# Attention, routing and experts on one core: counting the routing ranks before the output rows, and four other changes of order

## The reference

```
x = layernorm(x + attention(x))       # causal, 16 query heads, 4 key/value heads of 128
x = layernorm(x + ffn(x))

ffn: logits = clip(x @ gate_w.T, -50, 50)            # 8 experts
     top 2 of the logits, rw = softmax of these two
     deltas = softmax(expert_atom_weights) @ atoms ; weighted = deltas * sigmoid(importance)
     each expert adds 4096 scattered entries (positions mask_idx) to the shared matrix W
     out = x @ W.T + sum over the two experts of rw * (their sparse part applied to x)
```

## Time and profile before

| | |
|---|---|
| median of 3 runs | 1902.2 us (1900.52 to 1905.72) |
| the profiled execution | 1894.24 us |
| its span, first to last instruction | 1892.5 us |
| mean granted TensorE clock | 0.981 |
| busy: PE, DVE, ACT, POOL | 92%, 69%, 43%, 41% |
| HBM | 203 GB/s over the span |

### The profile page before, as it was taken

One profiled execution on the slowest core, in us unless ns is written; L12 is line 12 of the kernel. 1 busy time (PEld: TensorE's weight loads), 2 busy tenths in 40 slices (PEclk: granted clock), 3 DMA queues, 4 the chain that ended last, 5 costly groups with the idle time before them and its releaser, 6 DMA issues.

```text
span 1892.5 us, 33146 instructions
## 1 busy us (share of the span) xinstructions
PE 1744.0 (92%) x8750; PEld 1455.4 (77%) x8750; DVE 1313.9 (69%) x4043; ACT 814.2 (43%) x1950; POOL 777.1 (41%) x1093
## 2 busy tenths in 40 slices
PE   8999989998999999999999899999999999999983
PEld 7888877787777777777778777777777778777862
DVE  5566467766777688758876788768776787773356
ACT  4444434434444344434444444444443443434454
POOL 6775444434443322223322333133322224675564
PEclk9999999999999999999999999999999999999997
DMA  9655555555555666556665666576665747544698
GB/s 320 228 206 201 180 174 171 177 159 195 168 168 162 212 210 211 184 187 182 213 201 166 206 211 207 183 232 201 201 195 194 257 134 289 196 156 153 242 313 322
DMA packets 195148, 386.41 MB, mean 204 GB/s; under 512 B 27328, under 2 KB 98144, under 8 KB 184480
## 3 DMA queue, kind: packets, MB, share of 16 engines
q1 hardware_dynamic: 176688, 344.53, 54.0%
q0 software_dynamic: 18288, 39.80, 6.7%
HBM read 261.64 MB, written 122.62 MB: 203 GB/s over the span
## 4 chain that ended last, share of the span: by engine, by line
PE 60%; DVE 15%; issue 10%; ACT 7%; DMA 4%; POOL 2%; DVEq 1%; SPq 1%; ACTq 0%; POOLq 0%
PE psum L1598 17%; PE psum L1600 16%; PE psum L1599 16%; ACT probs L1897 5%; PE psum L1626 4%; DVE probs_blocks L2060 3%; DMA token_rows<-x,ids_now 2%; PE psum L2457 2%; PE psum L2458 2%; PE psum L2459 2%; DVE y_acc L2099 1%; DVE route_product L700 1%; PE psum L376 1%; DMA route_rows<-attn_residual 1%; DVE route_stats L682 1%
## 5 line engine op out<-in xcount | busy, mean ns | idle before, releaser
L1471 POOL TENSOR_SCALAR probs<-probs,row_inv 128x128 f32<-128x128 f32 (+3 forms) x512 | 284.9, 581 | 514.4 <-DVE row_inv L2045 514.1
L1897 ACT ACTIVATE probs<-probs,neg_max 128x512 f32<-128x512 f32 (+3 forms) x512 | 282.0, 553 | 430.6 <-DVE neg_max L2037 429.7
L1598 PE MATMUL psum<-xT_hi,w_hi 128*128 128x512 f32 x640 | 257.4, 402 | 7.8 <-DVE xT_lo L785 3.9
L1600 PE MATMUL psum<-xT_hi,w_lo 128*128 128x512 f32 x640 | 250.8, 392 | 0.0
L1599 PE MATMUL psum<-xT_lo,w_hi 128*128 128x512 f32 x640 | 250.2, 391 | 0.0
L2037 DVE CUSTOM_DVE_ANT_0 probs<-psum,causal 128x512 f32<-128x512 f32 (+3 forms) x512 | 221.3, 487 | 27.3 <-issue 14.2
L1598 PE MATMUL psum<-kT_hi,qT_hi 128*128 128x512 f32 (+3 forms) x512 | 176.4, 345 | 54.6 <-DVE qT_lo L2085 54.6
L1598 PE MATMUL psum<-wo_hi,oT_hi 128*128 128x512 f32 x496 | 198.0, 399 | 26.1 <-DVE y_acc L2099 26.1
L1600 PE MATMUL psum<-wo_hi,oT_lo 128*128 128x512 f32 x496 | 195.4, 394 | 0.0
L1599 PE MATMUL psum<-wo_lo,oT_hi 128*128 128x512 f32 x496 | 194.9, 393 | 0.0
L1599 PE MATMUL psum<-kT_lo,qT_hi 128*128 128x512 f32 (+3 forms) x512 | 169.4, 331 | 0.0
(11 more groups left out here) (255 smaller groups left out, 4037.2 us busy)
## 6 DMA issues: line engine op xcount, KB each, us to landing
w_hi<-split_qk_weights SPq DMA_DIRECT2D x140, 256.0 KB, 3.9
w_lo<-split_qk_weights SPq DMA_DIRECT2D x140, 256.0 KB, 4.8
probs_strips<-probs_blocks SPq DMA_DIRECT2D x54, 640.0 KB, 3.0
probs_moved<-probs_strips SPq DMA_DIRECT2D x216, 160.0 KB, 3.3
wo_hi<-split_out_weights SPq DMA_DIRECT2D x27, 1024.0 KB, 6.5
wo_lo<-split_out_weights SPq DMA_DIRECT2D x27, 1024.0 KB, 8.7
expert_weights_hi_lo<-split_expert_weights SPq DMA_DIRECT2D x8, 2048.0 KB, 10.2
x_in<-in_L_attn_x_dram SPq DMA_DIRECT2D x8, 1024.0 KB, 6.1
```

The lines of the kernel that those rows point to most:

```text
L1471: last = pool.tensor_scalar(p, p, row_inv[:, buf, i:i + 1], 1.0, ALU.mult, ALU.mult)
L1598: pe.matmul(dst, hi_s, hi_m, start=start, stop=False)
L1600: return pe.matmul(dst, lo_s, hi_m, start=False, stop=stop)
L1897: last = act.activation(probs[:, buf, a:a + w], probs[:, buf, a:a + w], ACT.Exp, bias=neg_max[:, buf, i:i + 1], scale=-1.0, accum_out=row_ ...
```

## The change

Ranks and sums: in `first` and `group` iterations of routed batches PE issues `route_ranks` before row 0 instead of after it, and DVE does `route_shares`, `route_ranked` and `route_places` before it adds row 0. The low part of a piece goes from DVE to POOL, after `normalize(n + 4, 0)` and before `route_place`. In every routed iteration but the last, `turn_blocks(n, it, 0)` stands before `qT(n + 2, 0)` on DVE. In `first` iterations of routed batches, variance, normalizing and the first three logits stand behind the maxima of the fourth head, and ACT copies the moved probabilities before it copies the third value row.

More of the change, by code:

```diff
@@ L1851, in iteration @@
                 sum_entries(pe, N, psum, BANKS_PT[0], QUADS_OF[g])
[L1852 to L1855, removed]
+            if route and kind == "batch":
+                ranks()
             if kind == "batch":
@@ L2077, in pT @@
                 low(pT_lo[:, buf, a:z], pT_hi[:, buf, a:z], psum[:, BANKS_PT[u], 0:z - a], s_pt_lo)
-        def low_piece(b, g):
-            dve.wait_ge(s_piece_hi, piece_number(b, g) + 1)
-            low(F.piece_lo[:], F.piece_hi[:], F.piece_raw[:].rearrange("p (r e) -> p e r", e=NE), s_piece_lo)
         def qT(n, buf, bank):
@@ L2180, in iteration @@
                 add_rows(it - 1, 2, "group")
-            if late:
+            if late and not moved:
                 route_normalize(dve, R, tt)
@@ L2198, in iteration @@
                 moved_pT(n, 0)
-            if late:
+            if late and not moved:
                 route_logits(dve, R, tt, (1, 2), products)
+            if late and moved:
+                route_variance(dve, R, tt)
             if kind == "batch" and not moved:
@@ L2277, in iteration @@
                 table_numbers(dve, E, table)
[L2278 to L2284, removed]
+            def ranked():
                 if job == "last" and g == 0:
@@ L2292, in iteration @@
                 route_ranked(dve, R, tt, BANKS_PT[0])
+            if moved and kind != "batch":
+                route_shares(dve, R, tt)
+                ranked()
+                route_places(dve, R, tt)
+            if kind == "first" and route:
+                wait_apart(dve, s_seed, b + 1, s_passed)
+            add_rows(it, 0, banks)
             if kind in ("batch", "end"):
+                add_rows(it, 1, kind)
+                if route:
+                    route_shares(dve, R, tt)
+                    ranked()
                 add_rows(it, 2, kind)
-            if route:
+                if route:
+                    route_places(dve, R, tt)
+                add_rows(it, 3, kind)
+            elif route and not moved:
+                route_shares(dve, R, tt)
+                ranked()
                 route_places(dve, R, tt)
-            if kind in ("batch", "end"):
-                add_rows(it, 3, kind)
         run(dve, iteration)
```

## The result

The changed kernel takes 1883.4 us (median of 5 runs, 1880.9 to 1890.5) against 1902.2 us before: a ratio of 0.991, 95% interval 0.988 to 0.993. It is faster by 0.9%, or 18.8 us, three times the 0.3% that the prediction named as what a measurement can tell from no change. The forecast was 1906 us, no change, with a range of 1892 to 1920, and the result lies under it. The profiled execution took 1885.93 us (span 1884.2, granted clock 0.980).

The account below looks back on a forecast made before the run. PE, busy 92%, was taken to be bound by its waits for low queries and row sums. Terms -26 - 5 + 3.6 + 44 + 3 - 15 = +4.6 us gave 1906 us on the 1902.2 median, range 1892 to 1920.

Parts of the forecast that it names:

- the first groups were to give back: In seven first iterations, two overlapping delays return 2.2 us each time, 15.4 us of the 30.5 us gained.
- the late logits: First iterations: eight logits behind the fourth head's maxima make the low key and first low output late, about 652.1 against 650.5.
- the late second move: First iterations: SP's store waits for later normalized rows, so strips queued behind it are moved by 655.5, wanted at 653.6.
- Blocks before the low query: Transposes fill DVE's 1.81 us idle time, so row 1's sum comes earlier and 20 PE waits end: -26 us, clock -5.
- The clock's part (-5): In the batch iterations of batches 3 and 4, two close waits lower PE's clock; ending them saves 5 us, bounds 0 and -6.
- First groups: Seven first iterations: low query no longer behind variance, normalizing and a logit; -30.5 plus 15.4 returned, -15 us (bounds -28, -5).
- Small operations first: Ahead of row 0's sum, they meet POOL's normalizing; maxima 0.45 us late in 8 iterations without a split piece: +3.6 us.
- The piece on GpSimd: Holds DVE's second rank product, delaying maxima 3.4 us in 12 iterations: +44 us, plus 3 in four batch iterations.
- D: Duration of the piece's low part on POOL, not in the trace: taken as 3.3 us, between 2.4 and 4.4.
- Rival A: Small operations aren't held by the piece on POOL: -37 us, 1865 us; chance 0.2.
- C: Rival: POOL's piece takes 2.4 us whatever the stride, first iterations give nearly all back: -21 us, 1881 us; chance 0.18.
- B: Rival: the stride lengthens POOL's piece to 4.4 us, holding the second rank product in 12 iterations: +25, 1927 us; chance 0.17.

Follow-up runs that it names:

- the first pair: First profiled executions of the kernel before and of the changed kernel; attention (first instruction to last transposes of probabilities) took 1592.24 and 1578.33 us.
- the second profile: Changed kernel profiled again, unaltered, on the chip where the kernel before was profiled again; ratio 0.990 to the kernel before.
- blocks and first groups: Kernel before with the block transposes ahead of the low query and the late variance in first iterations, nothing else; ratio 0.970.
- piece on VectorE: Changed kernel with the low part of the piece back on VectorE, between the low outputs of the last two heads; ratio 0.970 to the kernel before.
- the blocks alone: Kernel before with only the block transposes moved ahead of the low query; ratio 0.969.
- the late variance alone: Kernel before with only the late variance of the first iterations and ScalarE's new order; ratio 0.993.
- the early load: Kernel before with one SyncE edit: in first iterations the load of the rows is issued ahead of the blocks' move; ratio 0.987.
- GpSimd's quarters: Changed kernel with the piece's low part at its place on GpSimd, cut into four instructions of two experts each; ratio 0.987 to the kernel before.
- the early piece: Changed kernel with the piece's low part on GpSimd, but ahead of the split of the values; ratio 0.970 to the kernel before.

## Why the prediction was wrong, point by point

The recorded sum is +4.6 us; attention showed -13.9 in the first pair and -18.0 in the second profile. The runs split the -13.9 exactly along the sum's terms:

| terms | forecast | measured | from |
|---|---|---|---|
| blocks and first groups | -26 - 5 - 15 = -46 | -55.5 | blocks and first groups |
| small operations, beside these | +3.6 | +0.7 | piece on VectorE, less the row above |
| piece on GpSimd, beside these | +44 + 3 = +47 | +40.9 | changed, less piece on VectorE |
| sum | +4.6 | -13.9 | |

Each is a difference of single profiles, which repeat to some 4 us. The signs were right; sizes were off, and most of all one.

**The step that failed** is what the first groups were to give back: "together I count 2.2 us in each: 7 x 2.2 = 15.4". Measured it is 5.0 us beside the blocks (the 20 iterations take 35.9 us less with the blocks alone and 30.9 with the late variance added) and 7.7 without them. PE's waits in the changed kernel say about the same, some 6 us: 5.6 for POOL's low values (2.4 before) and 2.7 for low probabilities (none before). Which of the two delays, the late logits or the late second move, was counted too high, no run separates. This one term is 10 us of the 18.5 by which the sum was off; the piece is 6, the blocks in their 20 iterations 5, small operations 3, all to the same side. Against them stand the 30.5 us of the first groups' waits, of which 26.0 came, and small rests.

*Blocks before the low query* (-26 and -5): the mechanism was right, and the size nearly so in the 20 iterations (-36 us). Its reach was not: the forecast counted the transposes on VectorE but not what waits for them in SyncE's queue in the first groups: strips, four moves, and behind these the load of the rows. That is 23 us for the blocks alone. It didn't move this sum, since the late variance ends the same stall and the sum had that already under first groups. The clock's part (-5) was laid to two close waits in two `batch` iterations; the late variance alone and the early load keep both waits (27.4 us for rows' sums in all) and have the 2.1 us each as well, so that cause isn't shown.

*First groups* (-30.5 given, 15.4 given back, -15): the forecast had the right chain ahead of the low query ("variance, which waits for its rows, normalizing and a logit") and changed the order of it, without asking why the rows came late: their load stood behind the blocks. The gain isn't the late variance's alone: beside the blocks it is worth nothing (-55.5 against -59.3), and without them 22.4 us, 4.2 of which I give to no edit.

*Small operations first* (+3.6): a wrong inference of little weight. The first product is held as I said (0.48 us), but the sum and the operations only change places: maxima start no later, PE waits 0.3 us for row 0's sum and 1.2 instead of 1.5 for the low query. Unseen was the `end` iteration, where PE does row 1 straight behind the scores, with no query projection between, and so meets row 0's sum 3.25 us early: +4.8 in that iteration alone, +3.1 in the change.

*The piece on GpSimd* (+44 and +3): right in mechanism and place. D was 3.03 us where I took 3.3; PE's wait 2.7 to 2.9 where I had 3.6, and the clock fell behind only eight of the 12. Taken out of the changed kernel it is 40.9 us, added alone 42.2, against 47. Rival A is out. The Trainium skill's exclusive lock ("SBUF — State Buffer", section "Who interferes with whom") agrees with these traces, by the 2.81 and 2.87 us of L746; its slower strided reads ("GPSIMD Engine Reference", section "Performance pitfalls for Q7 kernels") gave an estimated 3.3 us against the 3.03 measured.

*The rivals.* C's number (1881) came near the 1883.4 measured, and that is luck: its piece was to cost 34 us (and its sum leaves out the +3 of the `batch` iterations) and cost 40.9, its first groups were to give 28 and gave 21 (26.0 less 5.0), and the blocks gave 5 more than all theories had. B needed D over 3.4.

## What to carry to other kernels

When an engine's operation is moved earlier, follow what its result triggers on the DMA queues, and what is queued behind that: here the place of one load, which the change had not touched, was 25 us. Two edits that each end a stall are worth the stall once, so run each part alone before crediting it. An operation given to GpSimd needs a place where it holds nobody; here the same instruction was nearly free beside VectorE's work on PSUM and cost 41 us beside small operations in SBUF.

## What the hardware showed that was not expected

GpSimd's subtraction of two SBUF tensors holds VectorE's operations on SBUF even where these have one input and two columns: L748, L754 and L755 took 0.65 to 0.72 us instead of 0.17 while GpSimd's quarters (3.45 us for four) ran. Under the normalizing, a `TENSOR_SCALAR` of GpSimd, the one-input L731 had run in 0.14 us; it has one column instead of two, and no run tells whether that or GpSimd's operation makes the difference. Cutting the long instruction didn't help: each small operation waited for one quarter. The operations with a PSUM input that ran beside the early piece weren't held (0.69 us under the 3.11 us piece).

GpSimd's subtraction with one input read at a stride of eight elements took 3.00 to 3.23 us for 1024 columns, about 3.0 ns a column; contiguous, give 1288 ns for 512, 2.5 ns a column.

Waits of PE of nearly the same length (2.83 and 2.73 us) were followed by a granted clock of 0.57 and of 1.00 over the next 4 us. Seven of the 12 such waits are of 2.73 us: four of these were followed by 0.50 to 0.63, three by 1.00. The length of a stall alone didn't tell which.
